# An adaLN block with differential attention on one core: the work ahead of the first exponential is laid out anew

## The chip, the cores and the metric

The kernel runs on one core of a Trainium2 chip. The metric is the device time of one execution in microseconds (us); the median over three runs counts. TensorE (PE) does the matrix products, VectorE (DVE), ScalarE (ACT) and GpSimd (POOL) the elementwise work, and SyncE (SP) issues nearly all DMAs.

## The reference, cut to what matters

The input x has 4 batch elements of 2048 tokens and 256 features. There are 32 score heads of width 8 (16 heads, two softmaxes each).

```
mod = (silu(c) @ wmod).reshape(4, 6, 1, -1)
sa, ca, ga, sb, cb, gb = (mod[:, k] for k in range(6))
ga, gb = (2 * (g >= 0) - 1) * maximum(abs(g), 0.25) for both gates
h = layernorm(x) * (1 + ca) + sa
q, k, v = h @ Wq.T * 8 ** -0.5, h @ Wk.T, h @ Wv.T          # 32, 32 and 16 heads
aw = softmax(q k^T)                                        # [32, 2048, 2048] for each element
attn = rmsnorm((aw[even] - lam * aw[odd]) @ v) * subln_w * (1 - LAMBDA_INIT)
x = x + ga * (attn @ Wo.T)
h = layernorm(x) * (1 + cb) + sb
x = x + gb * (h @ (ternary(Wf) * scale).T)
```

## The kernel before, in words

**Tiles and loops.** A batch element's 2048 tokens are taken in four chunks of 512, and its 32 score heads in eight groups of four. The main loop has 16 bodies of two groups each, four for each batch element. A body issues 256 exponentials (L644), each over 128 keys by 2 heads by 512 queries; PE makes the scores of each (L744) and adds the weighted values (L758) two steps behind. The scores lie in three slots of PSUM, so PE can be at most three exponentials ahead of ACT.

**Splits.** Queries and keys are stored as sums of three bf16 parts: the head (the value rounded), the middle (the rest rounded), and the low part. A query row also gets three rows with the split of an upper bound of its scores, the *maxima*, so that the exponential needs no running maximum. Everything passes through DRAM: `q_scr`, `k_scr`, `v_scr` for the split chunks, `m_scr` for the maxima; a group's rows are loaded from there into `queries`, `keys` and `values` (two buffers each).

**Beside the main loop.** While batch element b is in the main loop, PE, DVE, POOL and SP also make the chunks of element b+1 (kind "a" in `steps_of`, in places written out by hand) and the outputs of element b-1 (kind "e"). ACT does nothing there but exponentials. Batch element 0 has no earlier element to hide behind: its four chunks are made ahead of the main loop, and that stretch is what the change lays out anew. I call it the opening.

**The opening before.** SP loads c, the lambdas, wmod, the first chunk of x and the five weights (L420 to L427). PE makes the modulation as rows, 4 by 1536 (L653); DVE edits them (L916 to L924), SP stores them to `mod_scr` (L429), and loads them back as columns, one feature in each partition (`a_cols`, L347). DVE also makes the ternary weight (L930 to L932) and clears what it must, and then adds to `setup_done`; PE waits for it ahead of the first transpose. Then, for each chunk: transposes (L664), DVE's evacuation with the modulation (L969), queries and keys (L678), values (L670), DVE's evacuations (L971, L974) and its maxima and minima (L951 to L956). The split goes hand over hand: ACT writes the head (L635), POOL subtracts (L587), ACT writes the middle (L637), POOL the low part (L589), and only then does ACT take the next of the four pieces. `a_qk`, `a_parts` and `a_v` exist once. So ACT's first head of a chunk waits until all 13 stores of the chunk before have landed. Behind the fourth chunk come the bounds (L728), DVE's reductions and split (L1060 to L1081), four transposes (L715), DVE's copies (L1069), the stores to `m_scr` (L412) and the loads of the maxima (L405). SP loads the first group's rows (L392, L398) once the last chunk is stored.

**At a change of batch element** PE reads a flag that says whether the bounds are good enough (L780). If they are not, PE makes exact maxima in a long block of instructions; the trace shows no instruction of it, so PE always branches over it.

Of the kernel before, what the change touches and what calls it, by code (L numbers as in the profile page):

```python
# [7 lines left out]
ALU = mybir.AluOpType  # L8
# [4 lines left out]
P = 128  # L13

# [23 lines left out]
def adaln_diff_attention(nc, x, wqT, wkT, wvT, woT, lq1, lk1, lq2, lk2, subln, wfT, cT, wmod, out):  # L38
    B, T, E = x.shape
    HD = lq1.shape[0]  # L40
    VD = 2 * HD
# [44 lines left out]
    CRIT = M_STEPS - 1  # L86
# [22 lines left out]
    def steps_of(body):  # L109
# [11 lines left out]
        if b < B - 1:  # L121
            put("a", body + NC, A_TURN if turn else [spread(i) for i in range(A_STEPS)])
# [22 lines left out]
    GROUP_LOADS = 2 * 2 + 2 + 1  # L145
    ROW_LOADS = 2 * 2
# [7 lines left out]
    m_scr = nc.dram_tensor("m_scr", [B, PARTS, NS, T], BF16, kind="Internal").ap()  # L154
    attn_scr = nc.dram_tensor("attn_scr", [B, E, T], F32, kind="Internal").ap()
    mod_scr = nc.dram_tensor("mod_scr", [B, 6, E], F32, kind="Internal").ap()

    with ExitStack() as ctx:
# [16 lines left out]
        mod_sb = sb("mod_sb", [B, 6, E])  # L175
# [34 lines left out]
        a_cols = sb("a_cols", [P, 2, EC])  # L210
# [17 lines left out]
        e_cols = sb("e_cols", [P, 2, EC])  # L228
# [19 lines left out]
        m_split = sb("m_split", [P, NB, PARTS, NS], BF16)  # L248

        m_rest = w_low[:, :, :].rearrange("p c (n s) -> p (c n) s", s=NS)  # L250
        m_parts = wmod_sb[0:PARTS * NS, :, :].rearrange("p c f -> p (c f)").bitcast(BF16)[:, 0:T]

# [14 lines left out]
        consts_set = sem("consts_set")  # L267
        ident_set = sem("ident_set")
        weights_loaded = sem("weights_loaded")
        wmod_loaded = sem("wmod_loaded")  # L270
        small_loaded = sem("small_loaded")
# [3 lines left out]
        mod_product = sem("mod_product")  # L275
# [3 lines left out]
        w_total = sem("w_total")  # L279
# [14 lines left out]
        a_cols_loaded = sem("a_cols_loaded")  # L294
        a_head = sem("a_head")
        a_rest_done = sem("a_rest_done")
        a_middle = sem("a_middle")
# [41 lines left out]
        def _(sp):  # L339
# [4 lines left out]
            def a_columns(b):  # L344

                for c in range(EC):
                    sp.dma_start(a_cols[:, :, c], mod_scr[bass.ds(b, 1), 0:2, c * P:(c + 1) * P].rearrange("o k p -> p (o k)"), allow_slow_non_contiguous=True).then_inc(a_cols_loaded, DMA)  # L347

            def a_store_qk(job, b, tc, i):

                sp.wait_ge(a_split, (job + 1) * 4 + i + 1)
                c = i % 2
                for first, n in ROW_RUNS:
                    part = QK_ROWS[first]
                    if i < 2:
                        src = a_parts[:, i, part[0]:part[0] + 1, :].broadcast_to([P, n, CH])
                    else:
                        src = a_parts[:, i, 0:n, :]
# [17 lines left out]
            def e_modulation(b):  # L376
# [3 lines left out]
                for i, kind in enumerate((2, 5)):  # L380
                    sp.dma_start(e_gate[:, i, :], mod_scr[bass.ds(b, 1), kind, :].broadcast_to([P, E])).then_inc(e_mod_loaded, DMA)
# [795 lines left out]
```

## Time and profile before

| | us |
|---|---|
| median of three runs (3962.2 to 3964.03) | 3962.35 |
| profiled execution | 3960.17 |
| its span, first to last instruction | 3958.4 |
| first exponential starts | 141.70 |
| ACT busy, share of the span | 3780.8, 96% |
| PE busy, share of the span | 3756.7, 95% |
| DVE busy; POOL busy | 1199.6; 635.7 |
| granted TensorE clock, mean | 0.987 |

The page gives busy times as shares of the whole span. Two engines at 95% and more say little of which one is waited for; that is read from the waits and the timeline. The tenth of the span in which the opening lies differs from all others: PE's busy digit is 6 in the first of 40 slices and 9 later, ACT's is 1.

### The profile page before, as it was taken

What the parts mean: (1) busy time and instruction counts of PE and PEld (TensorE: products, weight loads), DVE (VectorE), ACT (ScalarE), POOL (GpSimd) and SP (SyncE); (2) the same over time, 40 slices, a digit from 0 to 9 for tenths busy, and PEclk for the clock granted to TensorE, in tenths of its full rate; (3) what the DMA queues carried; (4) which work ended last, traced back from release to release, by engine and by line L of the source; (5) the groups of instructions that cost most, each with busy time, mean ns of one, the idle gap of its engine ahead of it and who ended that gap; (6) DMA issues with size and microseconds to landing.
All of it is one profiled execution on the core that took longest, in us unless ns stands there. A gap on an engine that the chain in (4) does not pass through costs nothing.

```text
span 3958.4 us, 74927 instructions
## 1 busy us (share of the span) xinstructions
PE 3756.7 (95%) x32082; PEld 951.4 (24%) x32082; DVE 1199.6 (30%) x2778; ACT 3780.8 (96%) x4132; POOL 635.7 (16%) x402
## 2 busy tenths in 40 slices
PE   6699999999999999999999999999999999999997
PEld 3222212222222222222222222222222222211122
DVE  7332322223232332332422332322432213212133
ACT  1699999999999999999999999999999999999995
POOL 5121212112020121211111120211200101001011
PEclk8799999999999999999999999999999999999999
DMA  5412112211122212122221211221111110301101
GB/s 175 110 38 52 35 41 49 49 25 46 34 62 50 49 47 59 35 47 59 48 49 46 50 54 41 54 59 42 46 34 39 42 41 14 60 3 25 35 19 40
DMA packets 134503, 188.35 MB, mean 48 GB/s; under 512 B 15172, under 2 KB 109124, under 8 KB 133960
## 3 DMA queue, kind: packets, MB, share of 16 engines
q1 hardware_dynamic: 134152, 183.35, 19.0%
q8 instruction: 260, 4.26, 0.5%
q14 instruction: 91, 0.75, 0.1%
HBM read 97.82 MB, written 85.48 MB: 46 GB/s over the span
## 4 chain that ended last, share of the span: by engine, by line
ACT 58%; issue 28%; PE 11%; DMA 1%; POOL 1%; DVE 1%; SPq 0%; POOLq 0%; DVEq 0%; ACTq 0%
ACT probs L644 57%; PE ps L758 6%; PE ps L744 3%; PE ps L670 1%; DMA v_scr<-a_v 1%; PE ps L678 1%; POOL a_parts L589 0%; POOL a_rest L587 0%; DMA m_scr<-wmod_sb 0%; PE ps L664 0%; ACT a_parts L637 0%; DMA w_o<-in_woT_dram 0%; PE ps L728 0%; SPq L359 0%; DVE normed L886 0%
## 5 line engine op out<-in xcount | busy, mean ns | idle before, releaser
L644 ACT ACTIVATE probs<-ps 128x1024 f32<-128x1024 f32 x4096 | 3760.1, 1493 | 40.5 <-PE ps L744 39.4
L758 PE MATMUL ps<-probs,values 128*32 128x512 f32 x16384 | 2186.8, 606 | 8.2 <-DVE seg_t L1008 3.6
L744 PE MATMUL ps<-queries,keys 64*128 64x512 bf16 x8192 | 1467.5, 386 | 125.6 <-DMA queries<-m_scr 23.7
L618 POOL TENSOR_TENSOR seg_rs<-seg_ms,neg_half 64x16 f32<-64x16 f32 x128 | 370.5, 2894 | 2909.3 <-DVE seg_ms L1017 2909.3
L744 PEld LDWEIGHTS ps<-queries,keys 64*128 64x128 bf16 x8192 | 374.7, 92 | 1863.7 <-ACT probs L644 1583.3
L758 PEld LDWEIGHTS ps<-probs,values 128*32 128x32 f32 x16384 | 322.6, 108 | 572.3 <-issue 500.2
L1008 DVE STREAM_TRANSPOSE seg_t<-ps 128x512 f32<-128x512 f32 x128 | 91.8, 717 | 868.3 <-PE ps L758 868.3
L994 DVE TENSOR_TENSOR e_tmp<-ps,e_gate 128x512 f32<-128x512 f32 x64 | 44.1, 689 | 450.5 <-PE ps L670 450.5
L1021 DVE TENSOR_TENSOR seg_n<-seg_d,seg_rs 64x256 f32<-64x256 f32 x128 | 62.7, 490 | 386.5 <-POOL seg_rs L618 386.5
L971 DVE TENSOR_SCALAR a_qk<-ps 128x512 f32<-128x512 f32 x64 | 44.2, 691 | 345.0 <-PE ps L678 344.7
L1025 DVE SCALAR_TENSOR_TENSOR seg_a<-seg_n,subln_sb 32x256 f32<-32x256 f32 x256 | 133.9, 523 | 6.0
L664 PE MATMUL ps<-ident,normed 128*32 128x128 f32 x2048 | 100.3, 286 | 19.5 <-DVE stats L941 10.4
L664 PEld LDWEIGHTS ps<-ident,normed 128*32 128x32 f32 x2048 | 69.0, 116 | 146.5 <-issue 145.9
L969 DVE TENSOR_SCALAR a_hT<-ps,a_cols 128x512 f32<-128x512 f32 x32 | 25.6, 808 | 220.0 <-PE ps L664 220.0
L678 PE MATMUL ps<-a_hT,w_q 128*32 128x256 f32 x1024 | 79.2, 405 | 13.2 <-DVE a_hT L969 13.2
L1029 DVE STREAM_TRANSPOSE seg_o<-seg_a 32x512 f32<-32x512 f32 x128 | 89.5, 700 | 4.4
L670 PE MATMUL ps<-w_f,e_hT 128*32 128x256 f32 x1024 | 78.1, 388 | 6.9 <-DVE e_hT L991 6.8
L670 PE MATMUL ps<-w_o,e_attn 128*32 128x256 f32 x1024 | 77.5, 379 | 1.4 <-DMA e_x<-in_x_dram 1.3
L678 PE MATMUL ps<-a_hT,w_k 128*32 128x256 f32 x1024 | 73.5, 379 | 0.0
L670 PE MATMUL ps<-w_v,a_hT 128*32 128x256 f32 x1024 | 73.5, 379 | 0.0
L974 DVE COPY a_v<-ps 128x256 f32<-128x256 f32 x64 | 23.7, 416 | 156.6 <-PE ps L670 155.0
L991 DVE TENSOR_SCALAR e_hT<-ps,e_cols 128x512 f32<-128x512 f32 x32 | 25.7, 805 | 144.8 <-PE ps L664 144.8
(116 smaller groups left out, 1176.5 us busy)
## 6 DMA issues: line engine op xcount, KB each, us to landing
queries<-q_scr SPq DMA_DIRECT2D x64, 384.0 KB
keys<-k_scr SPq DMA_DIRECT2D x64, 384.0 KB
v_scr<-a_v SPq DMA_DIRECT2D x16, 1024.0 KB, 4.5
values<-v_scr SPq DMA_DIRECT2D x32, 512.0 KB
q_scr<-a_parts SPq DMA_DIRECT2D x32, 384.0 KB, 2.6
k_scr<-a_parts SPq DMA_DIRECT2D x32, 384.0 KB, 2.6
a_x<-in_x_dram SPq DMA_DIRECT2D x16, 512.0 KB, 12.7
q_scr<-a_parts SPq DMA_DIRECT2D x32, 256.0 KB, 2.9
```

What stands on the lines that cost most here:

```text
L618: nc.gpsimd.tensor_tensor(seg_rs[:, :], seg_ms[:, :], neg_half[0:64, :], ALU.pow).then_inc(seg_rs_done, 1)
L644: nc.scalar.activation(probs[:, u % PRING, n % PAIRS, :, :], slots[slot_of(body, n)], ACT.Exp).then_inc(exp_done, 1)
L664: last = nc.tensor.matmul(bank[j:j + 32, n * P:(n + 1) * P], src[:, n, c * P + j:c * P + j + 32], ident[:, :], start=True, stop=True)
L670: last = nc.tensor.matmul(bank[j:j + 32, (n % 2) * E:(n % 2 + 1) * E], hT[:, c, n * P + j:n * P + j + 32], w[:, c, :], start=(c == 0), sto ...
L678: last = nc.tensor.matmul(bank[j:j + 32, t], w[:, c, f * P + j:f * P + j + 32], hT[:, c, t], start=(c == 0), stop=(c == EC - 1))
L744: last = nc.tensor.matmul(slots[slot_of(body, n)][:, half, :], keys[buf][at:at + KS_ROWS, n % PAIRS, blk * P:(blk + 1) * P], queries[buf][ ...
L758: last = nc.tensor.matmul(pv[j:j + VW, :], values[buf][:, blk, half, :], probs[:, u % PRING, pair, half, :], start=(blk == 0), stop=(blk = ...
L971: last = V.tensor_scalar(a_qk[:, i - 2, :], bank, SCALING if i < 4 else 1.0, None, ALU.mult)
L1008: V.transpose(seg_t[:, :, :].rearrange("p c d -> p (c d)"), pv).then_inc(pv_read, 1)
L1021: V.tensor_tensor(seg_n[:, :, :], seg_d[:, :, :], seg_rs[:, :].rearrange("p (c o) -> p c o", o=1).broadcast_to([64, NQ, VD]), ALU.mult).th ...
L1025: last = V.scalar_tensor_tensor(seg_a[:, :, h * VD:(h + 1) * VD], seg_n[q, :, :], 1.0 - LAMBDA_INIT, subln_sb[q, :].rearrange("p (o d) -> ...
L1029: V.transpose(seg_o[:, :], seg_a[:, :, :].rearrange("p c d -> p (c d)")).then_inc(seg_done, 1)
```

## The change

What it does, part by part; numbers in brackets are used in the text below.

(1) *Modulation.* PE makes the columns themselves, eight small products with wmod as the stationary side, for the first two kinds ahead of the first transpose and for kinds 3 and 4 behind the bounds. The gates stay rows. Of wmod the first third is loaded by itself, the first chunk of x goes ahead of it, and ACT's queue issues the loads of Wq, Wk and Wv. The ternary weight, the gates and the lambdas move behind the fourth chunk, and PE no longer waits for `setup_done` ahead of the first transpose. POOL clears two of four row buffers later, and by 32-bit words.

(2) *Evacuation and split.* In the opening ACT evacuates the transposes (`turned`) and the queries and keys (`projected`), and sums the keys on the way. `hT`, the rest and the parts are double-buffered, the second `parts` in `probs`. POOL's subtraction of piece i goes ahead of its low part of piece i-1, and ACT's head of piece i ahead of its middle of i-1. PE transposes chunk tc+1 between the keys and the values of chunk tc.

(3) *First rows.* SP loads the first group's rows of chunk tc-1 in the middle of chunk tc.

(4) *Maxima.* `m_scr` and `m_split` have the head outermost, so a head's three rows are neighbours in `m_parts`, and SP loads them from there (`first_maxima`) at the opening and at each change of batch element; in the opening ACT copies them out of PSUM. The stores to `m_scr` remain, behind it. The flag's bound is now taken ahead of the split.

(5) *The branch.* PE gets a prefetch hint for the branch over the exact block, half a block of 16 units ahead of each change of batch element and once in the opening.

(6) In body 0 the steps of kind "a" stand eight units later.

```
+            turned(0)
+            for tc in range(NC):
+                projected(tc, 0)
+                for i in range(1, 4):
+                    projected(tc, i)
+                    middle(tc, i - 1)
+                if tc < NC - 1:
+                    turned(tc + 1)
+                middle(tc, 3)
...
+            for tc in range(NC):                            # POOL
+                if tc < NC - 1:
+                    a_power(tc + 1)
+                rest(tc, 0)
+                for i in range(1, 4):
+                    rest(tc, i)
+                    low(tc, i - 1)
+                low(tc, 3)
...
+            def projected(tc, i):
+                act.wait_ge(p_projected, tc * 4 + i + 1)
+                if tc > 0:
+                    act.wait_ge(p_rest_done, (tc - 1) * 4 + i + 1)
+                    act.wait_ge(p_bounded, (tc - 1) * 4 + i + 1)
...
+                if tc > 1 and i == 0:
+                    act.wait_ge(p_stored[tc % 2], 4 * len(ROW_RUNS) * DMA)
...
+            def first_rows(tc):                             # SP
+                sp.wait_ge(p_stored[tc % 2], (tc // 2 + 1) * (4 * len(ROW_RUNS) * DMA))
+                sp.wait_ge(p_v_stored, (tc + 1) * DMA)
...
-            group_rows(0, 0, 0)
-            m_stores(0)
-            group_maxima(0, 0, 0)
+            first_rows(NC - 1)
+            sp.wait_ge(p_maxima, NC)
+            first_maxima()
+            m_store(0, m_stored)
...
-                with pe.If(exact > 0):
+                pe.br_lt(exact, 1, on_true=f"pe_ready_{b}", on_false=f"pe_exact_{b}").branch_hint(skip_hint)
...
-            put("a", body + NC, A_TURN if turn else [spread(i) for i in range(A_STEPS)])
+            put("a", body + NC, A_TURN if turn else [spread(i + (body == 0)) for i in range(A_STEPS)])
```

PE's queue in the opening, where the first chunk ends and the second begins. Before (`w_q`, `w_k`, `w_v` are the weights):

```order
L678 MATMUL ps<-a_hT,w_k 32x256 x32
L670 MATMUL ps<-w_v,a_hT 32x256 x32
L664 MATMUL ps<-ident,normed 32x128 [waits a_normed]
L664 MATMUL ps<-ident,normed 32x128 x31
L678 MATMUL ps<-a_hT,w_q 32x256 [waits a_evacuated]
```

And now:

```order
L771 MATMUL ps<-a_hT,w_k 32x256 x32
L757 MATMUL ps<-ident,normed 32x128 [waits p_turned_read,a_normed]
L757 MATMUL ps<-ident,normed 32x128 x15
L757 MATMUL ps<-ident,normed 32x128 [waits p_turned_read]
L757 MATMUL ps<-ident,normed 32x128 x15
L763 MATMUL ps<-w_v,a_hT 32x256 x32
L771 MATMUL ps<-e_hT,w_q 32x256 [waits p_projected_read,p_turned_read]
```

The transposes moved ahead of the values, so the values lie between them and the product that needs their evacuation.

SP's queue in the opening, from the last store of a chunk on. Before, with what follows the fourth chunk (three stores for each of four pieces and one of `a_v` make up a chunk):

```order
L364 DMA v_scr<-a_v 128x8x256 [waits a_evacuated]
L347 DMA a_cols<-mod_scr 128x2x1 x2
L342 DMA a_x<-in_x_dram 128x4x256
L392 DMA queries<-q_scr 48x2x2048 [waits a_stored]
L392 DMA keys<-k_scr 48x2x2048
L392 DMA queries<-q_scr 48x2x2048
L392 DMA keys<-k_scr 48x2x2048
L398 DMA values<-v_scr 128x1024
L412 DMA m_scr<-wmod_sb 96x512 [waits m_evacuated] x4
L405 DMA queries<-m_scr 3x4096 [waits m_stored]
```

Now, from the second chunk's second piece on; the five loads stand in each chunk but the first, and once more at the end:

```order
L381 DMA q_scr<-probs 128x3x512 [waits a_split]
L381 DMA q_scr<-probs 128x2x512
L381 DMA q_scr<-probs 128x512
L420 DMA queries<-q_scr 48x2x512 [waits p_v_stored,p_stored0]
L420 DMA keys<-k_scr 48x2x512
L420 DMA queries<-q_scr 48x2x512
L420 DMA keys<-k_scr 48x2x512
L427 DMA values<-v_scr 128x256
L370 DMA a_x<-in_x_dram 128x4x256 [waits a_normed]
L381 DMA k_scr<-probs 128x3x512 [waits a_split]
```

The loads of the first group moved into the chunks; the load of x and the stores of the keys now stand behind their wait.

PE's queue eight units ahead of the first change of batch element, now (the scores of a unit are four products, its weighted values four more; before, the same rows stand without the hint):

```order
L851 MATMUL ps<-probs,values 32x512 [waits exp_done]
L851 MATMUL ps<-probs,values 32x512 x3
L952 BRANCH_PREFETCH_HINT
L837 MATMUL ps<-queries,keys 128x512 [waits exp_done]
L837 MATMUL ps<-queries,keys 128x512
```

Only the hint is new; the read of the flag and the branch stand behind the body's last unit as before.

## Rows read from the trace of the kernel before

**Rows 1.** The page, busy time of each engine.
```profile
PE 3756.7 (95%) x32082; PEld 951.4 (24%) x32082; DVE 1199.6 (30%) x2778; ACT 3780.8 (96%) x4132; POOL 635.7 (16%) x402
```

**Rows 2.** Waits of ACT: us in total, times, longest.
```profile
ACT probs L644 <- PE ps L744: 39.4, 12, 26.9
```

**Rows 3.** Timeline of ACT from the first exponential: start, duration, [idle before].
```profile
141.70 939.57 ACT L644 ACTIVATE probs<-ps 128x1024 f32<-128x1024 f32 x1024 [26.89 <-PE ps L744]
...
1083.91 1.94 ACT L644 ACTIVATE probs<-ps 128x1024 f32<-128x1024 f32 x2 [2.64 <-PE ps L744]
...
3907.54 7.84 ACT L644 ACTIVATE probs<-ps 128x1024 f32<-128x1024 f32 x8 [0.34 <-PE ps L744]
```

**Rows 4.** Timeline, all engines, from the start to the first store.
```profile
11.41 8.20 PE L653 MATMUL ps<-wmod_sb,silu 128*4 128x512 f32 x12 [11.41 <-DMA wmod_sb<-in_wmod_dram]
...
17.53 1.41 DVE L875 BATCH_NORM_STATS2 stats<-a_x 128x6 f32<-128x256 f32 x4
...
20.69 1.38 DVE L886 TENSOR_SCALAR normed<-a_x,moments,a_rstd 128x256 f32<-128x256 f32 x4 [1.14 <-POOL a_rstd L568]
...
30.34 3.64 PE L664 MATMUL ps<-ident,normed 128*32 128x128 f32 x64 [10.40 <-DVE stats L941]
...
34.90 3.66 PE L678 MATMUL ps<-a_hT,w_q 128*32 128x256 f32 x64 [0.92 <-DVE a_hT L969]
...
41.57 2.41 SPq L359 DMA_DIRECT2D q_scr<-a_parts  x3
```

**Rows 5.** Timeline, two chunks of the opening.
```profile
60.08 0.63 ACT L635 ACTIVATE a_parts<-a_qk 128x512 bf16<-128x512 f32 x1 [8.94 <-DMA v_scr<-a_v]
...
62.69 1.16 POOL L589 TENSOR_TENSOR a_parts<-a_rest,a_parts 128x512 bf16<-128x512 f32 x1 [0.74 <-ACT a_parts L637]
...
63.67 1.92 PE L664 MATMUL ps<-ident,normed 128*32 128x128 f32 x64
...
73.91 3.63 PE L678 MATMUL ps<-a_hT,w_k 128*32 128x256 f32 x64
```

**Rows 6.** Timeline, DVE's normalisation with POOL busy, and with POOL idle.
```profile
39.10 2.52 DVE L886 TENSOR_SCALAR normed<-a_x,moments,a_rstd 128x256 f32<-128x256 f32 x4
...
75.30 1.38 DVE L886 TENSOR_SCALAR normed<-a_x,moments,a_rstd 128x256 f32<-128x256 f32 x4
```

**Rows 7.** Timeline of SP's queue, last store to the maxima's loads.
```profile
117.81 0.67 SPq L364 DMA_DIRECT2D v_scr<-a_v  x1
...
123.81 0.35 SPq L392 DMA_DIRECT2D queries<-q_scr  x1
...
126.49 1.87 SPq L412 DMA_DIRECT2D m_scr<-wmod_sb  x4
138.40 0.56 SPq L405 DMA_DIRECT2D queries<-m_scr  x2
```

**Rows 8.** Stretches: from:to, length, each engine's busy time, PEclk, DMA share, GB/s.
```profile
0.00:17.00 17.00, 5.58 (x7) 0.86 (x8) 2.79 (x6) 1.79 (x4) 15.96 (x17) 1.00 0.63 202
60.00:81.00 21.00, 17.53 (x336) 10.18 (x332) 19.27 (x41) 5.01 (x9) 10.55 (x9) 0.92 0.70 227
75.00:78.00 3.00, 3.00 (x60) 1.67 (x56) 2.93 (x9) 0.00 (x0) 0.00 (x0) 1.00 1.03 339
1005.00:1010.00 5.00, 4.62 (x36) 0.95 (x34) 0.00 (x0) 5.00 (x7) 0.00 (x0) 1.00 0.73 141
1010.00:1015.00 5.00, 4.75 (x48) 1.32 (x45) 0.46 (x1) 5.00 (x7) 0.00 (x0) 1.00 1.05 160
1015.00:1020.00 5.00, 5.00 (x52) 1.51 (x52) 2.67 (x9) 5.00 (x7) 0.00 (x0) 1.00 1.02 233
```

**Rows 9.** Timeline of DVE, the maxima of batch element 0.
```profile
104.29 0.70 DVE L1042 TENSOR_TENSOR box_w<-head_mask,box 128x80 bf16<-128x80 f32 x4
...
116.12 2.47 DVE L1069 CAST wmod_sb<-ps 96x512 bf16<-96x512 f32 x4
```

**Rows 10.** Timeline of PE at the first change of batch element.
```profile
1083.27 1.04 PE L744 MATMUL ps<-queries,keys 64*128 64x512 bf16 x4 [3.30 <-issue]
```

More of the change, by code:

```diff
@@ L342, in a_load, with store_qk @@
                 sp.dma_start(a_x[:, :, :], x[bass.ds(b, 1), bass.ds(tc * CH, CH), :].rearrange("o (n p) e -> p (o n) e", p=P)).then_inc(a_loaded, DMA)
[L344 to L351, printed above, removed]
+            def store_qk(parts, b, tc, i, stored):
                 c = i % 2
@@ L548, in _ @@
             nc.gpsimd.tensor_copy(ident_bf[:, :], ident[:, :]).then_inc(ident_set, 1)
-            for buf in range(2):
-                nc.gpsimd.memset(keys[buf][:, :, :], 1.0).then_inc(consts_set, 1)
-                nc.gpsimd.memset(queries[buf][:, :, :], 0.0).then_inc(consts_set, 1)
             nc.gpsimd.memset(head_mask[:, :], 1.0).then_inc(ident_set, 1)
@@ new lines, in _ @@
+            for i in range(M_BOUNDS):
+                m_step(0, i, ps[:, i, :])
+            skip_hint = pe.mark_branch_hint_location()
+            pe.wait_ge(p_valued_read, NC * 2)
+            pe.wait_ge(wmod_rest_loaded, DMA)
+            pe.wait_ge(w_sum_done, 1)
+            pe.wait_ge(consts_set, 8)
+            columns((3, 4), ps[:, 6, :])
+            nc.tensor.matmul(ps[:, 6, 2 * EC * B:2 * EC * B + 1], ones[:, :], w_sum[:, :], start=True, stop=True)
+            for n, kind in enumerate((2, 5)):
+                for c in range(EC):
+                    last = nc.tensor.matmul(ps[0:B, 7, n * E:(n + 1) * E], silu[:, c, :], wmod_sb[:, c, kind * E:(kind + 1) * E], start=(c == 0), stop=(c == EC - 1))
@@ L775, in _ @@
+            last.then_inc(late_product, 1)
+            m_step(0, CRIT, ps[:, 4, :])
+            for k in range(NC):
+                m_step(0, CRIT + 1 + k, ps[:, k, :])
+            pe.wait_ge(p_maxima, NC)
+            pe.wait_ge(cols_done, 2)
+            pe.wait_ge(setup_done, 1)
+            pe.wait_ge(out_loaded, 2 * DMA)
             exact_runs = pe.alloc_register("pe_exact_runs")
@@ new lines, in _ @@
+            m_sizes(mlink)
+            for i in range(CRIT + 1):
+                m_evacuate(mlink, 0, i, ps[:, (0, 1, 2, 3, 4, 5, 4)[i], :])
+            assert mlink.count == M_LINKS, mlink.count
+            V.memset(m_mean[:, :], 0.0).then_inc(m_evacuated, NC)
+            dve.wait_ge(late_product, 1)
+            link.then(V.tensor_scalar(w_scale[:, :], ps[:, 6, 2 * EC * B:2 * EC * B + 1], 1.0 / (E * E), 1e-5, ALU.mult, ALU.max))
+            columns(2, ps[:, 6, :])
+            V.tensor_copy(mod_sb[:, :, :].rearrange("b k e -> b (k e)"), ps[0:B, 7, :])
```

473 lines of the change are left out of this document (280 added, 193 removed).

## The prediction, made before the changed kernel ran

> **What bounds the kernel now.** I read the page's busy times first, then who waits for whom, then the timeline. On the page ACT is busy 96% of the span and PE 95% [rows 1]; shares alone don't say which is waited for. ACT's timeline does: from 141.70 on the first batch element's 1024 exponentials take 939.57 us without a gap, 0.918 us each [rows 3], though PE does all projections of the next element beside them. So the exponentials set the pace, and work beside them costs nothing while PE keeps its slots full. What is left is time in which ACT has no exponential: ACT waited for PE twelve times, 39.4 us in all, 26.9 of it in one wait [rows 2], which is the end of the opening. The other 12.5 us are at the three changes of batch element, but for three small waits at the run's end such as the 0.34 us one [rows 3], some 0.9 together: 11.6 us at the changes, 2.64 of them in the first gap [rows 3]. What follows the last exponential isn't touched by more than the source of two columns. So the change can take time from two places: the 141.7 us of the opening, and the 11.6 us.
>
> **The opening, its start.** The first transpose runs at 30.34, though its input (the normalised chunk) was there at 22.07, for it waited for DVE's clearing [rows 4]. Part (1) takes that wait away, moves x to the front and sends three weights by ACT's queue. From the start of the statistics to the normalised chunk is 22.07 - 17.53 = 4.5 us [rows 4]. When x is there is not shown; the first 17 us moved 202 GB/s [rows 8], and c, x and the first third of wmod are 1.05 MB, so 5.2 us for these alone and 9.1 with the 0.79 MB of the other queue beside them. I take 7.5, and the transposes at 12, 18.3 us earlier. The modulation columns lie beside this: eight small products must beat the 8.20 us that PE took for the rows [rows 4]; if they took all of that from 8 on, they would be 2 to 3 us late. Range 10 to 16.
>
> **The opening, the chunks by compute.** Before, ACT's second head of a chunk had to wait for POOL, and its first 8.94 us for the last store to land [rows 5]. Now the pieces overlap and the buffers are double. PE has per chunk 3 x 3.63 us of products (q, k, v; only k's is shown) and 1.92 of transposes, 12.8 us [rows 5]. POOL has 8 x 1.16 + 1.0 = 10.3 [rows 5]. DVE was busy 19.27 us in a chunk of 21 [rows 8] and loses two evacuations of the transposes, four of queries and keys and two sums, all 512 columns wide; at 0.7 us (a fourth of the four 512-column copies' 2.47 us is 0.6 [rows 9]) these are 5.6, so 13.7 stay. PE and DVE are thus near each other, 13.7 us a chunk. The first query product follows the transposes by 34.90 - 30.34 = 4.6 [rows 4], so at 16.6; the fourth chunk's at 16.6 + 3 x 13.7 = 57.7; its queries, keys and values end 3 x 3.63 later, at 68.6. From the weights of the bounds to DVE's last copy was 116.12 + 2.47 - 104.29 = 14.3 us [rows 9]; ACT's copies don't change that by more than 1. From the issue of the maxima's two loads to the first exponential was 141.70 - 138.40 = 3.3 us [rows 3, 7]; four loads make it 4.1. By compute the first exponential stands at 87.0.
>
> **The opening, the chunks by DMA.** This is what I expect to be late next. A chunk's stores are four pieces of 128 x 6 x 512 bf16 and 1 MB of values, 4.19 MB. With the DMA engines full they moved 339 GB/s at a share of 1.03 [rows 8], 12.4 us a chunk. Between 60 and 81 us the share was 0.70 [rows 8]: there was room, and a chunk in 13.7 us takes it. The first group's rows were 2.1 MB; the stretch 1005 to 1020 holds such a load and one chunk of x and took 5 x (0.73 + 1.05 + 1.02) = 14.0 us of full engines [rows 8]; less 0.524 MB of x at 339 GB/s (1.5 us) that is 12.5, 3.1 for each chunk. They are slow by the byte: 160 GB/s at full share [rows 8]. Part (3) spreads them, it doesn't remove them, but only the last fourth is now behind the last store. So ahead of the last store's landing: 4 x 12.4 + 3 x 1.5 (x) + 3 x 3.1 = 63.4 us. The first store comes 41.57 - 30.34 = 11.2 us behind the first transpose [rows 4], at 23 to 24; data flow from 25. Landed: 25 + 63.4 = 88.4, with a gap or two 90; before, 123.81 [rows 7]. Then SP issues the last rows, 126.49 - 123.81 = 2.7 us [rows 7], and the maxima's loads, 4.1 us to the exponential: 96.8. Before, this last leg was 141.70 - 123.81 = 17.9 us, since the stores to `m_scr` stood behind the rows' loads (issued at 126.49, and their load only at 138.40 [rows 7]); part (4) takes that passage through DRAM away. DMA ends later than compute, so it decides: 96.8, 44.9 us earlier. Bounds: 84 if DMA is never the limit and DVE no slower than PE (87.0 - 3 x 0.9); 113 if stores go out at the pace of before, when the first went at 41.57 and the last at 117.81 [rows 4, 7]: 24 + 76.2 + 6 to land + 2.7 + 4.1.
>
> One thing may make the chunks longer. DVE's normalisation took 2.52 us where POOL worked beside it and 1.38 where POOL was idle [rows 6], 1.14 more, one POOL operation. Eight operations of this kind (four normalising, four making `q_sign`) could each wait once in a chunk: 8 x 1.16 = 9.3 us at most, as against the few waits that the 19.27 us already hold. I take 1 to 2 us more per chunk, which DMA covers: it has 9.8 us of slack over compute in four chunks. The Trainium skill, page SBUF — State Buffer, section Who interferes with whom, says that this pair of ports is an exclusive lock and that the second to come blocks for a whole instruction; the trace agrees, 1.14 against 1.16 us. By it the upper of the two numbers is possible, since POOL is now busy most of a chunk.
>
> **The changes of batch element.** PE issued nothing for 3.30 us at the branch [rows 10], and ACT, a little ahead of it by its slots, stood 2.64 us; the next scores then ran at 1.04 us for four matmuls, and ACT waited some more, until 11.6 us in three changes. Part (5) hints the branch. If the 3.30 us are the fetch of the target, they go, save for the read of the flag; I take 9 of 11.6 us. The trace has no hint, so the ends are 0 and 11.6. The Trainium skill, page Runtime: NRT & Kernel Launch, section Instruction fetch mechanics, says that fetch runs ahead in order only, and that a taken branch to a page not held must wait for a DMA. That agrees with a wait of 3.30 us with no releaser; it speaks of no hint, and by it alone nothing is gained here.
>
> **What costs nothing.** (6) and the moved loads of columns lie beside exponentials whose pace of 0.918 us hid such work already [rows 3]. What moved behind the fourth chunk (ternary weight, gates, lambdas) follows the maxima on DVE and must be done before the last rows land, 10 us later; without that cover it would cost its few us. In the opening the branch lies under the DMAs.
>
> **Sum.** The profiled execution is 3960.17 us, 1.77 more than its span. 3960.17 - 44.9 - 9 = 3906.3. The median of the runs is 2.2 us above the profiled one: 3908.5, I say 3908.
>
> **The rivals.**
> *Hint without effect* (chance 0.22). For: PE may wait at the read of the flag and not for instructions; the trace can't tell. Against: no releaser is named. 3908.5 + 9 = 3917.
> *DMA isn't the limit* (0.12). For: loads in pieces of 1 KB may go at 339 GB/s, as stores do (3 x 1.6 us saved), and the stores may start earlier. Against: the 160 GB/s. First exponential at 86 to 90, 3898 to 3902.
> *POOL and DVE block each other* (0.18). If all eight operations wait, 13.7 + some 6 = 19.7 a chunk: 16.6 + 3 x 19.7 + 10.9 + 14.3 + 4.1 = 105; or SP's one queue, in which the stores of keys and the load of x now stand behind the wait for the chunk before, delays both, up to 113. 3917 to 3925.
> *Slower* (0.03). The exact block. Bounds now come from sums taken by ACT and in another order; if a bound of one element rose above 80, the flag would be set. Then DVE reduces 512 times over 2048 columns, each at least 4 x 0.6 us by the copy [rows 9]: 1.2 ms, about 5100 us. It decides from one flagged element on. Against: only rounding differs, and the trace has no instruction of that block. *No change* (0.03): the opening as long as before for a reason I don't see.
>
> **How the numbers follow.** My forecast, DMA-bound with a hint that works, has 0.42 (3902 to 3914). The range for 8 in 10 takes in the missing hint and most of the blocked case: 3898 to 3922. A measurement of this kernel tells 0.2%, about 8 us, from no change; every case but the last two lies 37 us or more below. Faster 0.94, same 0.03, slower 0.03.
>
> **What would show it.** The first exponential at about 97, and a DMA share near 1 from 30 to 90 us; the last `v_scr` store landed about 90; gaps of ACT under 1 us at the changes. Wrong, if ACT's first exponential comes with DMA share well under 0.9 in the chunks (then compute or SP's order is the limit), if PE still shows an idle time of 3 us there, or if the exponentials take more than 0.92 us.

## The result, and the profile after

| | before | after |
|---|---|---|
| median of the runs | 3963.19 us (3962.2 to 3964.97) | 3916.55 us (3916.12 to 3917.69, 4 runs) |
| ratio to before, with its 95% interval | 1 | 0.9883 [0.987, 0.9895] |
| profiled execution, its span | 3960.17, 3958.4 us | 3916.22, 3914.5 us |
| first exponential | 141.70 us | 108.32 us |
| ACT's waits for scores, the first left out | 12.5 us | 1.6 us |

The kernel is 46.6 us faster. The forecast was 3908, with a range of 3898 to 3922: the time is inside it, 8.5 us above the forecast. The span is 43.9 us shorter: 33.4 in the opening (forecast 44.9) and 10.5 behind the first exponential (forecast 9). The 10.5 are a difference: from the first exponential to the ones behind ACT's last gap it takes 3753.8 us instead of 3765.8, 12.0 less, and what follows them takes 52.4 instead of 50.9, 1.5 more. The last product of PE is the reason for the 1.5:

```profile
3904.00 5.54 PE L763 MATMUL ps<-w_f,e_hT 128*32 128x256 f32 x64 [0.92 <-DVE e_hT L1124]
```

In the kernel before, the same product took 3.66 us, at a granted clock of 0.95 (3949 to 3953). Here, from 3904 to 3908, the granted clock was 0.52, near the lower of its two levels (1.2 GHz). PE had done the same just before in both, transposes of 3.64 us behind an idle time of 6.26, so why the clock was lower here is not shown.

Waits of ACT in the kernel after (us in total, times, longest), which answers to [rows 2]:

```profile
ACT probs L736 <- PE ps L837: 11.4, 6, 9.8
```

Its timeline from the first exponential to the last gap (start, duration, count, idle before), which answers to [rows 3]:

```profile
108.32 5.61 ACT L736 ACTIVATE probs<-ps 128x1024 f32<-128x1024 f32 x6 [9.83 <-PE ps L837]
114.29 1.94 ACT L736 ACTIVATE probs<-ps 128x1024 f32<-128x1024 f32 x2 [0.36 <-PE ps L837]
116.53 3657.09 ACT L736 ACTIVATE probs<-ps 128x1024 f32<-128x1024 f32 x3986 [0.30 <-PE ps L837]
...
3862.13 7.83 ACT L736 ACTIVATE probs<-ps 128x1024 f32<-128x1024 f32 x8 [0.34 <-PE ps L837]
```

From 116.53 on 3986 exponentials run without one gap, over all three changes of batch element; 3657.09 / 3986 = 0.917 us each, the pace of before. The 1.6 us of waits that are left lie elsewhere: 0.66 right behind the first exponential, and the same 0.93 at the run's end as before. Nothing that was laid beside them cost time.

The opening's timeline, all engines, chosen rows, which answer to [rows 4] and [rows 5]:

```profile
10.13 6.21 DVE L1021 TENSOR_SCALAR normed<-a_x,moments,a_rstd 128x256 f32<-128x256 f32 x4 [1.21 <-POOL a_rstd L608]
...
16.49 3.64 PE L757 MATMUL ps<-ident,normed 128*32 128x128 f32 x64 [4.59 <-DVE normed L1021]
...
28.69 4.19 SPq L381 DMA_DIRECT2D q_scr<-a_parts  x6
32.92 0.64 SPq L370 DMA_DIRECT2D a_x<-in_x_dram  x1
38.31 1.41 DVE L1010 BATCH_NORM_STATS2 stats<-a_x 128x6 f32<-128x256 f32 x4 [3.82 <-DMA a_x<-in_x_dram]
40.41 1.11 POOL L608 TENSOR_TENSOR a_rstd<-a_ve,neg_half 128x4 f32<-128x4 f32 x1 [5.64 <-DVE a_ve L1015]
41.63 4.78 DVE L1021 TENSOR_SCALAR normed<-a_x,moments,a_rstd 128x256 f32<-128x256 f32 x4
46.47 3.64 PE L757 MATMUL ps<-ident,normed 128*32 128x128 f32 x64 [6.14 <-DVE normed L1021]
...
64.76 3.44 PE L757 MATMUL ps<-ident,normed 128*32 128x128 f32 x64 [3.89 <-DVE normed L1021]
```

Two things are to be seen. The first normalisation took 6.21 us, where 1.38 was its time with POOL idle [rows 6], and the transposes start at 16.49 instead of 12. And PE then stands still twice, 6.14 and 3.89 us, for the normalised chunk (I call these places the seams): SP issues the load of x only at 32.92, behind the six stores of queries; DVE's statistics wait for it until 38.31, POOL's power (which makes `a_rstd`, the factor of the normalisation) until 40.41, and four DVE operations take 4.78 us beside POOL's splits.

Stretches (length, busy time of PE, PEld, DVE, ACT and POOL, PEclk, DMA share, GB/s), which answer to [rows 8]:

```profile
30.00:90.00 60.00, 46.99 (x843) 31.90 (x835) 47.82 (x102) 27.39 (x52) 34.91 (x30) 0.89 0.88 287
75.00:85.00 10.00, 7.02 (x133) 3.69 (x125) 8.65 (x16) 6.18 (x14) 9.06 (x8) 1.00 1.07 368
99.00:103.00 4.00, 0.00 (x0) 0.00 (x0) 2.63 (x9) 0.00 (x0) 1.01 (x1) 0.50 0.22 59
```

Over the 60 us the DMA engines' share was 0.88, by stretches of 15 us 0.93, 0.88, 0.78 and 0.95: near full, with a dip where PE stands still at the second seam. The prediction's sign of being wrong was a share "well under 0.9"; 0.88 doesn't decide that. What does speak against the forecast is the first exponential, at 108.32 instead of about 97, and the last store. SP's queue at the end of the opening, which answers to [rows 7]:

```profile
93.30 0.68 SPq L385 DMA_DIRECT2D v_scr<-a_v  x1
99.52 0.34 SPq L420 DMA_DIRECT2D queries<-q_scr  x1
99.90 0.43 SPq L420 DMA_DIRECT2D keys<-k_scr  x1
100.38 1.91 SPq L420 DMA_DIRECT2D queries<-q_scr  x1
102.33 0.43 SPq L420 DMA_DIRECT2D keys<-k_scr  x1
102.80 0.43 SPq L427 DMA_DIRECT2D values<-v_scr  x1
103.28 2.91 SPq L452 DMA_DIRECT2D queries<-wmod_sb  x4
```

The last store landed at 99.5, since SP's wait for it ended then, not at 90; from there to the first exponential it is 8.8 us, not 6.8. So the 11.5 us that the opening misses are 4.5 (start) + 5.0 (chunks) + 2.0 (last leg). Counted from one store of values to the next, against before: the first store of values was issued 16.4 us earlier (38.88 for 55.30), the three chunks from there to the last took 54.4 instead of 62.5 us, and from the last one's issue to the first exponential it was 15.0 instead of 23.9.

### The profile page after: what moved, and what is told of

Same layout as the page of the kernel before. It is cut to its first block, busy times and chain, and to the rows that moved or that the text cites. A ratio compares the mean times of both kernels' runs of the same rounds, so it can differ in the third digit from the quotient of the medians.

```text
span 3914.5 us, 75013 instructions
## 1 busy us (share of the span) xinstructions
PE 3750.6 (96%) x32110; PEld 960.2 (25%) x32110; DVE 1188.5 (30%) x2745; ACT 3797.7 (97%) x4168; POOL 628.2 (16%) x402
## 4 chain that ended last, share of the span: by engine, by line
ACT 58%; issue 29%; PE 11%; DVE 1%; POOL 1%; SPq 0%; DMA 0%; ACTq 0%; POOLq 0%; DVEq 0%
ACT probs L736 58%; PE ps L851 5%; PE ps L837 3%; PE ps L763 1%; PE ps L771 1%; PE ps L757 0%; DVE normed L1021 0%; SPq L381 0%; PE ps L821 0%; SPq L420 0%; DMA v_scr<-a_v 0%; DMA a_x<-in_x_dram 0%; DVE seg_t L1141 0%; POOL a_rest L641 0%; POOL probs L647 0%
## 5 line engine op out<-in xcount | busy, mean ns | idle before, releaser
L1104 DVE TENSOR_SCALAR a_qk<-ps 128x512 f32<-128x512 f32 x48 | 33.2, 692 | 341.2 <-PE ps L771 341.2
L1102 DVE TENSOR_SCALAR a_hT<-ps,cols_sb 128x512 f32<-128x512 f32 x24 | 19.4, 810 | 213.7 <-PE ps L757 213.7
L1124 DVE TENSOR_SCALAR e_hT<-ps,cols_sb 128x512 f32<-128x512 f32 x32 | 25.7, 804 | 144.9 <-PE ps L757 144.9
L771 PE MATMUL ps<-a_hT,w_q 128*32 128x256 f32 x896 | 66.3, 379 | 1.0 <-ACT a_hT L692 1.0
## 6 DMA issues: line engine op xcount, KB each, us to landing
a_x<-in_x_dram SPq DMA_DIRECT2D x16, 512.0 KB, 12.9
```

What stands on the lines that cost most here:

```text
L771: last = nc.tensor.matmul(bank[j:j + 32, t], w[:, c, f * P + j:f * P + j + 32], hT[:, c, t], start=(c == 0), stop=(c == EC - 1))
```

## The experiments

Each is the kernel after with one edit, unless said otherwise. "Measured" gives the median with its range and the ratio to before with its 95% interval. Medians are to be read beside 3916.55, the profiled execution's first exponential beside 108.32.

Two things blur small differences. The kernel before, measured beside these runs, took 3959.7 us (the first four runs), 3962.86 (the next four), 3961.88 (the three after them) and 3963.31 (the last), and 3963.19 beside the kernel after; so medians of different groups can be compared to 3 or 4 us only. And the end of the run differs from kernel to kernel: what follows ACT's last gap took 52.4 to 52.9 us in the profiled executions of the kernel after and of the runs with clears late, values twice, and clears, x and maxima, whose last product of PE took 5.3 to 5.7 us, and 50.4 to 51.0 in all others, where it took 3.66. That has nothing to do with the edits as they were meant, and puts up to 2 us into the times. I therefore go by the traces' opening where a difference is small.

**The hint of the branch taken out.**

```
-  pe.br_lt(exact, 1, on_true=..., on_false=...).branch_hint(skip_hint)
+  pe.br_lt(exact, 1, on_true=..., on_false=...)
```

> The changed kernel without the branch hints, all else as it is. Theory (the idle time at the changes of batch element was the fetch of the branch's target): the idle time of PE of some 3.3 us comes back at each of the three changes, with the slow matmuls behind it, and the time rises by 9 to 12 us over the changed kernel's 3916.5, to 3926 to 3928. Rival (the gaps went for another reason, such as the earlier flag or the steps that moved): under 2 us. In the opening neither expects a difference, since the branch lies under the DMAs there; first exponential at 108.3.

Measured: 3927.59 us (3926.39 to 3931.68), ratio to before 0.9921 [0.9904, 0.9937], 11.0 more than with the hint, as the theory had it. ACT's waits, and PE at the first change of batch element:

```profile
ACT probs L736 <- PE ps L837: 22.0, 16, 6.9
```

```profile
1049.35 0.61 PE L837 MATMUL ps<-queries,keys 64*128 64x512 bf16 x4 [2.99 <-issue]
```

The idle time of [rows 10] is back, with no releaser, here and at the other two changes (3.42 and 2.93 us), and ACT's waits at the changes sum to 13.4 us, where they were 11.6 before and are none with the hint. The hint is the whole gain behind the opening; the rival by which PE waits at the read of the flag falls, for the flag is read in both. The Trainium skill, page Runtime: NRT & Kernel Launch, section Instruction fetch mechanics, lets a taken branch wait for the fetch of its target: the trace agrees, 2.99 us without the hint and no gap with it. By that page alone nothing was to be had.

**POOL's later clears behind the first normalisation.**

```
   a_power(0)
+  pool.wait_ge(a_normed, 1)
   clear(keys[1], ONE_PAIR)
```

> The changed kernel with one more wait: POOL's second block of clears comes behind DVE's first normalisation instead of beside it. Theory (DVE's four operations were held off by POOL's clears, one each): the normalisation takes 1.4 us instead of 6.2, the first transpose runs at 11.7 instead of 16.5, and if the DMAs or the chunks' own length set what follows, all of it moves with it: first exponential at 103 to 105, 3 to 5 us less in total. Rival (what sets the end is fixed by the load of the next chunk of x, which waits for the loads of the weights): the first exponential moves by under 1.5 us.

Measured: 3911.59 us (3911.05 to 3913.34), 0.9879 [0.9863, 0.9896]; 5.0 less. The normalisation and the transposes:

```profile
10.15 1.38 DVE L1022 TENSOR_SCALAR normed<-a_x,moments,a_rstd 128x256 f32<-128x256 f32 x4 [1.21 <-POOL a_rstd L608]
...
11.97 3.64 PE L758 MATMUL ps<-ident,normed 128*32 128x128 f32 x64
```

The four operations take 1.38 us again, the transposes start at 11.97, where the forecast had them, and the first exponential comes at 103.04, 5.3 earlier. That is what the theory expected, and the rival by which the load of x sets the end falls. In the kernel after, POOL's clears of 1.80, 1.80 and 1.95 us ran from 10.05 to 15.49, beside the four DVE operations: the first of these, begun at 10.13, ended at 13.74, just behind the second clear (13.59), and the next at 15.63, just behind the third. So a memset of POOL, too, holds DVE back until the whole instruction is done, and the first operation had to let two of them pass. The Trainium skill (SBUF — State Buffer, Who interferes with whom) states such a lock; the trace agrees, 6.21 against 1.38 us.

**The values stored twice** (the second time to a buffer that nobody reads; 1 MB more for each chunk, and the other engines' work as it was; whoever waits for the values' store waits for both).

```
   store_v(0, tc, p_v_stored)
+  sp.dma_start(v_twin[...], a_v[...]).then_inc(p_v_stored, DMA)
```

> The changed kernel with each chunk's values stored a second time, to a tensor that nobody reads: 1.05 MB or 3.1 us of full DMA engines more per chunk. Theory A (DMA is the limit through the whole opening): the first exponential comes 4 x 3.1 = 12.4 us later, at 120.7. Theory B (late loads of x and POOL's order hold the chunks, DMA only the end): the slack in the chunks takes half of it, 3 to 8 us, 111 to 116.

Measured: 3923.4 us (3921.4 to 3925.49), 0.9907 [0.989, 0.9923]; first exponential at 116.94, 8.6 later, DMA share from 30 to 90 us 0.93 at 306 GB/s. The 8.6 us can't all be put down to the second store, for part of them had come before one was issued:

```profile
21.74 5.64 PE L774 MATMUL ps<-a_hT,w_q 128*32 128x256 f32 x64 [0.98 <-ACT a_hT L695]
...
42.13 0.81 SPq L386 DMA_DIRECT2D v_scr<-a_v  x1
```

The first chunk's query product took 5.64 us, where it took 3.66 in the kernel after, and the first store of values went out at 42.13 instead of 38.88, 3.3 us later. The trace gives no reason for the long product; the granted clock was 1.00 in both. From that first store to the first exponential it was 74.8 us, 5.4 more than the 69.4 of the kernel after. So of about 12.4 us more of DMA work 5.4 came through, as theory B has it (3 to 8); the rest went into the gaps of the queues. DMA is near its limit but not at it.

**The first rows loaded at the end, as before: part (3) undone.**

```
-                        if tc > 0:
-                            first_rows(tc - 1)
...
-            first_rows(NC - 1)
+            for i in range(2):
+                sp.wait_ge(p_stored[i], 2 * (4 * len(ROW_RUNS) * DMA))
+            sp.wait_ge(p_v_stored, NC * DMA)
+            group_rows(0, 0, 0)
```

> The changed kernel with part (3) undone: the first group's rows are loaded whole behind the last store, as before. Theory A (DMA is full, so that spreading only moves its work): the last store of the values lands some 9 us earlier than 99.5, the rows take 12.5 us behind it, first exponential at 105 to 109, no change within 3 us. Theory C (spreading hides 9 us under the chunks): first exponential at 115 to 118, 7 to 10 us more in total. Theory B (the wait for the stores in the middle of SP's queue makes the load of x late): the idle times of PE at the ends of chunks, 6.1 and 3.9 us, shrink by more than half in the second.

Measured: 3915.91 us (3913.08 to 3918.17), 0.9892 [0.9875, 0.9908]; first exponential at 107.34. This is theory A's number, and theory C (115 to 118) falls: the part is worth nothing here. The last store of values is issued at 85.56, 7.7 us earlier than with the rows between, and the leg from there to the first exponential is 21.8 us instead of 15.0. The rows' bytes are in the way in one place or in the other. But the edit changes more than the place of the bytes. Without the rows ahead of it the last chunk of x is asked for 3.0 us earlier (49.20), and PE's second idle time falls from 3.89 to 1.93 us, as theory B expected. What the rows in the middle cost as bytes, and what they cost by holding up the load of x behind them, this run doesn't separate; nor was part (3) undone with x asked for early, where it may be worth something.

**The load of x behind the first split's stores.**

```
-  if i == 1: first_rows(tc - 1); wait; a_load(tc + 2)
+  if i == 0: wait; a_load(tc + 2)
+  if i == 1: first_rows(tc - 1)
```

> The changed kernel with the load of the next chunk of x issued by SP behind the chunk's first piece, no longer behind the second piece and the wait for the chunk before. Theory B (x comes late and holds DVE's statistics, with them POOL and the transposes): the loads are issued 2.5 to 5 us earlier, PE's idle times of 6.1 and 3.9 us at the chunks' ends fall by 2 to 4 each, and the first exponential comes 2 to 4 us earlier than 108.3, less than the idle times shrink, since DMA (a share of 0.88 from 30 to 90) takes part of it. Theory A (DMA is the only limit): the idle times shrink, the first exponential moves by under 1 us.

Measured: 3909.01 us (3908.19 to 3909.94), 0.9863 [0.9846, 0.9879]; 7.5 less. PE at the two seams:

```profile
43.56 3.50 PE L756 MATMUL ps<-ident,normed 128*32 128x128 f32 x64 [3.19 <-DVE normed L1020]
...
59.46 1.96 PE L756 MATMUL ps<-ident,normed 128*32 128x128 f32 x64 [1.92 <-DVE normed L1020]
```

x is asked for at 30.99, 44.38 and 60.59 instead of 32.92, 52.22 and 71.65, PE's waits are halved (from 10.0 to 5.1 us), the share from 30 to 90 us is 0.93, and the first exponential comes at 102.88, 5.4 earlier. Theory A (under 1 us) falls, and the gain is more than theory B's 2 to 4. Of the 5.4 the three chunks give 3.8 (50.6 us from the first to the last store of values, for 54.4) and the last leg 1.6 (13.5 for 15.0). The median's 7.5 hold another 2 that lie in the run's end (50.4 for 52.4 us) and not with x. SP's order was the larger part of the 5 us of the chunks.

**POOL's power for the next chunk behind two splits instead of ahead of them.**

```
-  if tc < NC - 1: a_power(tc + 1)    (ahead of rest(tc, 0))
+  if i == 1 and tc < NC - 1: a_power(tc + 1)    (behind low(tc, 0))
```

> The changed kernel with POOL's power for the next chunk behind the first low part, no longer ahead of the chunk's first subtraction. Theory B (the power waits for the statistics of a late x, and the splits wait behind it): POOL's idle times of 5.6 and 6.9 us ahead of the splits of chunks 1 and 2 go, the first stores of chunk 1 go out some 5 us earlier than 44.99, DMA is busier from 38 to 45 us, and the first exponential comes 2 to 5 us earlier. Rival (the splits lock out DVE's normalisation, which makes the transposes later still): the idle times of PE grow from 6.1 and 3.9 us, first exponential within 1 us or later.

Measured: 3923.29 us (3921.49 to 3925.52), 0.99 [0.9884, 0.9917]; first exponential at 115.86, 7.5 later. PE at the seams, of which there are now three:

```profile
33.97 3.64 PE L757 MATMUL ps<-ident,normed 128*32 128x128 f32 x64 [6.14 <-DVE normed L1021]
...
55.19 3.64 PE L757 MATMUL ps<-ident,normed 128*32 128x128 f32 x64 [6.15 <-DVE normed L1021]
...
76.09 3.64 PE L757 MATMUL ps<-ident,normed 128*32 128x128 f32 x64 [6.19 <-DVE normed L1021]
```

The edit was meant to take away POOL's 5.64 us of waiting in front of the splits, and the first exponential was to come 2 to 5 us earlier. A miss: the rival, by which PE's idle times grow, is what came. The power comes late, the normalisation behind it (29.13, again 4.78 us) too, and PE waits 6.1 to 6.2 us at each of three seams, where it waited at two. POOL's wait was the cheaper one.

**The maxima's copies ahead of the last rows.** SP's order is `first_maxima()`, then `first_rows(NC - 1)`.

> The changed kernel with the four loads of the maxima issued ahead of the wait for the last stores, no longer behind the last rows. The maxima are in SBUF at 98.5 and the last store has landed at 99.5, so the four issues (2.9 us) lie under the wait. Theory (SP's issues in a row are the last leg): the first exponential comes 2 to 3 us earlier, 105.3 to 106.3. Rival (the landing of the last rows, slow by the byte, is what ends last and the maxima's issues lay under it): under 1 us.

Measured: 3915.42 us (3914.03 to 3917.28), 0.988 [0.9863, 0.9896]. From the last store of values to the first exponential 12.9 us instead of 15.0, as the theory had it (2 to 3 us), but the first exponential at 108.35 in the profiled execution, whose last store of values went out 2.1 us later (95.44 for 93.30). That delay was there ahead of the edit's place: the first query product took 5.50 us instead of 3.66, and the first stores went out at 30.61 instead of 28.69. The median's 1.1 us less are undecided by themselves.

**Four edits together** (clears late, x early, power late, maxima first).

> The changed kernel with all four edits of these experiments: POOL's clears behind the first normalisation, the load of x early, POOL's power behind the first low part, the maxima's loads ahead of the last rows. If the gains added up: 5.3 (measured for the clears) + 3 + 3 + 2.5 = 14, first exponential at 94. Theory A, with DMA as the floor: the stores start at 24.4, 63 us of full DMA engines bring the last landing to about 89 at best, first exponential 96 to 98, time 3904 to 3907. Rival (DVE and POOL lock each other out more as they are packed closer): 100 or later, 3909 or more.

Measured: 3919.99 us (3918.18 to 3921.34), 0.9889 [0.9873, 0.9906]; first exponential at 114.42. A clear miss of theory A, by 13 to 16 us; the rival (100 or later, 3909 or more) holds. The late power spoils the others. With it x is asked for only after a normalisation that is itself late: at 29.85, 51.16 and 72.11, where the run with clears and x below has 28.39, 42.15 and 58.81.

**The maxima through DRAM at the start: part (4) undone there.**

```
-  first_maxima()
   m_store(0, m_stored)
+  sp.wait_ge(m_stored, NC * DMA)
+  group_maxima(0, 0, 0)
```

> The first group's maxima go out to DRAM with the four stores and are loaded back from there by two loads, as in the kernel before; the copies inside SBUF at the first group are gone, all else is as after. Theory A (the copies inside SBUF replace a store that must land and a load behind it, and this chain is the last leg before the first scores): the chain becomes four stores, their landing (some 4 us by the copies' own landing, 106.2 to 107.6 in the kernel after), two loads and their landing again, so the first exp comes 4 to 6 us later, at 112 to 114, and the run takes 3920 to 3923. Theory B (the rows of the last chunk, which stand ahead of the maxima in SyncE's program, land as late as the copies, so the maxima are not last): the stores overlap the rows' landing, the first exp moves by less than 2 us, and the run stays at 3916 to 3918.

Measured: 3917.26 us (3914.89 to 3918.95), 0.9888 [0.9871, 0.9904]. SP's queue, and the first scores:

```profile
103.27 1.88 SPq L457 DMA_DIRECT2D m_scr<-wmod_sb  x4
106.67 0.58 SPq L441 DMA_DIRECT2D queries<-m_scr  x2
...
109.24 1.04 PE L838 MATMUL ps<-queries,keys 64*128 64x512 bf16 x4 [11.31 <-DMA queries<-m_scr]
```

The way through DRAM costs 1.6 us of the first exponential (109.89) and nothing that the medians can tell: theory A (4 to 6 us) fails, theory B (under 2) holds. Before, from the issue of these stores to their load it was 11.9 us [rows 7], which the prediction put down to the passage; here it is 3.4. In those 11.9 us the DMA engines' share was 0.95 at 189 GB/s, with the rows' 2.1 MB issued just ahead. So they were in the main the rows' bytes, and they are short now because only a fourth of the rows is left there. That `m_scr` is also laid out otherwise was not tested apart.

**Clears and x together.**

> Two edits together that each took 5 to 7 us by themselves: the second clears on POOL wait for the first normed chunk, and the loads of x(tc + 2) are issued behind the stores of the chunk's first split instead of its second. Theory A (the two delays lie in a row, so they add): first exp 5.3 and 5.4 us earlier than 108.32, at 97.6, and 3904 to 3906. Theory B (the x loads come early enough only because the DMA queues are not full; with the whole stretch 4 us shorter they are, and the last stores land no earlier than the backlog lets them): the DMA share between the first store and the last is 0.97 or more, first exp 100 to 103, and 3906 to 3909.

Measured: 3905.64 us (3904.54 to 3908.96), 0.9859 [0.9843, 0.9876]; 10.9 less. First exponential at 100.33. Stretch:

```profile
30.00:90.00 60.00, 47.46 (x831) 31.63 (x823) 51.70 (x118) 26.87 (x53) 33.02 (x29) 0.91 0.95 314
```

8.0 of the 10.7 us add up in the first exponential. The 2.7 that don't were lost ahead of the chunks and not in full queues: the first query product took 5.84 us (3.66 with the clears alone), and the first stores went out at 26.75 instead of 24.18. From the first to the last store of values it is 50.5 us and from there to the first exponential 13.4, both as with x early alone. The two edits' gains thus add, which is theory A's mechanism: the median lies in its 3904 to 3906, and the share of 0.95 stays under theory B's 0.97. The first exponential stands among theory B's 100 to 103 only by what the start lost.

**Clears, x and the maxima's copies first.**

> The edits of the run with clears and x, and the copies of the maxima issued ahead of the last chunk's rows. Theory A (what the first scores wait for is the landing of whichever DMA is issued last, and the copies, 2 KB and slow to land, gain from going first): the leg from the last store of v to the first exp is 2 us shorter than with those two edits alone, and the run 1.5 to 2.5 us shorter. Theory B (the order of the two does not matter, since both must land and their sum is the same): within 1 us of the run with the two edits.

Measured: 3904.29 us (3902.53 to 3906.5), 0.9853 [0.9837, 0.987]. Share 0.96, first exponential at 98.13, and from the last store of values to it 11.7 us for 13.4. In the profile that is nearly the first theory (2 us); the medians differ by 1.4 us, with intervals that overlap. Its first query product took 5.51 us, too. It is the fastest version run, 12.3 us below the kernel after, and its first exponential is 1.3 us from the 96.8 that the forecast worked out for full DMA engines.

**A chunk split only when the one before has landed: the overlap undone.**

```
-  if tc > 1 and i == 0: act.wait_ge(p_stored[tc % 2], ...)
+  if tc > 0 and i == 0: act.wait_ge(p_stored[(tc - 1) % 2], ...); act.wait_ge(p_v_stored, tc * DMA)
```

> ACT's first piece of every chunk after the first waits until all stores of the chunk before have landed, as in the kernel before, though the buffers stay double; all else is as after. In the kernel after, the last store of a chunk was issued at 38.88, 57.85 and 78.04 and the next chunk's first piece was made at 35.84, 56.46 and 74.15. Theory A (the second buffer lets a chunk be split while the one before is still stored, and this carries the shorter chunks: 54.4 us from the first to the last store of values instead of 62.5): the first piece would have to wait until some 5 us behind the store of values, at 44, so each of the three chunks is 6 to 9 us longer, the first exp stands at 122 to 130, and the run takes 3930 to 3939. Theory B (each chunk already waits some 5 us at its seam for the normalised x, and the wait for the landed store lies beside that wait): 1 to 3 us a chunk, first exp 111 to 117, the run 3919 to 3926.

Measured: 3931.78 us (3929.09 to 3934.25), 0.9921 [0.9905, 0.9938]; first exponential at 122.94, 14.6 later. ACT's first pieces of the three chunks:

```profile
44.97 0.63 ACT L709 ACTIVATE probs<-a_qk 128x512 bf16<-128x512 f32 x1 [9.22 <-DMA v_scr<-a_v]
...
68.45 0.63 ACT L709 ACTIVATE a_parts<-a_qk 128x512 bf16<-128x512 f32 x1 [12.47 <-DMA v_scr<-a_v]
...
93.58 0.63 ACT L709 ACTIVATE probs<-a_qk 128x512 bf16<-128x512 f32 x1 [13.86 <-DMA v_scr<-a_v]
```

Both numbers lie in theory A. The wait of [rows 5] is back, and the share falls to 0.75. From the first store of values to the last it is 70.4 us (38.78 to 109.14), 16.0 more, while the last leg gets 1.2 shorter. Of the parts undone here this is the largest; part (1), behind which the first store of values goes out 16.4 us earlier than before, was not undone.

## Why the prediction was right, and where 8.5 us went

**Right: what bounds the kernel.** The exponentials' pace didn't move (0.917 us), and both places named gave all that was gained. The time is in the range, and the sign of the gain is as forecast, 46.6 us of 54. But the forecast's own case, a first exponential at about 97 and 3902 to 3914 us, did not come. The time is inside by the width of the range, which was taken to hold most of the blocked case.

**Right: the changes of batch element.** Taken as 9 us of 11.6; all 11.6 came, for no gap is left at a change. A part had been left standing for the read of the flag, and ACT shows no gap for it. The exponentials beside those gaps, which had been slower, add 1.1, and new waits behind the first exponential take 0.7 off; that makes 12.0, so the term was too small by 3.0; the slower end of the run takes 1.5 of them back.

**Wrong by 4.5 us: the start.** The transposes were set at 12 with 4.5 us from the start of the statistics to the normalised chunk, a duration from a time when POOL was idle [rows 4, 6]. But the change moves POOL's clears to just that place. The prediction counted the lock for the chunks, at one POOL operation of 1.16 us each, and not here, where the operations are memsets of 1.8 us. The move of the clears brought 4.5 us back.

**Wrong by 5.0 us: the chunks.** The step that failed is "which DMA covers: it has 9.8 us of slack over compute in four chunks", that is, that DMA's time hides what DVE and SP lose. It takes the bytes as one block that only has to be pushed through. They come in bursts: PE stood 6.14 and 3.89 us, stores came late for it, and the share was 0.88. The rival "POOL and DVE block each other", which has SP's queue order in it as well (0.18, first exponential at 105 to 113, 3917 to 3925) named both mechanisms; the first exponential at 108.32 is its number, the time 3916.55 lies just under it. x asked for earlier brought 3.8 us of it back in the chunks, and 1.6 in the last leg. The other half of PE's waits is argued only: PE waited for the normalisation each time, and that took 4.78 and 3.81 us where 1.38 is its time with POOL idle, 5.8 more in two seams. That this lock takes the rest of a seam was not separated: the one edit that tried to move POOL's operations made it worse. With clears, x and maxima mended the share is 0.96 and the first exponential at 98.13. So the DMA bound is borne out to 1.3 us by that version, and the kernel as changed didn't reach it.

**Wrong by 2.0 us: the last leg.** The issue of the rows took 3.7 us instead of 2.7, since one of the loads took 1.91 (at most 0.43 for the others). And from the first of the maxima's four loads to the first exponential it was 5.0 us instead of 4.1; that term came from a row in which all other loads had landed, while here the rows' bytes are still under way. The copies issued first make it shorter by 1.7 to 2.1 us.

**Right in sum, wrong in its reason: parts (3) and (4).** The leg did fall by 8.9 us against before. The prediction put this down to the last fourth of the rows and to the passage through DRAM. Undone alone, neither costs anything the medians can tell (3915.91 and 3917.26 against 3916.55). Part (3) moves 7 us from the leg into the chunks; part (4) is worth 1.6 us, and the 11.9 us of [rows 7] that it was to remove were in the main the rows' bytes. What carries the opening is the overlap of part (2), 14.6 us, and, by the trace alone, the earlier start of part (1). Whether each is worth more in before than when undone here was not tried.

**The medians.** The profiled execution is 0.3 us below the median here, where 2.2 were added. With the terms above: 3906.3 + 11.5 - 3.0 + 1.5 = 3916.3, measured 3916.22.

## What to carry to other kernels

A total of DMA time is a bound for a stage only if the queues are fed all the time: follow one chunk through the program of the engine that issues, and look where the load for the next chunk stands behind stores that wait for this one. When an engine's work is moved, price its neighbour on the shared port at the new place, not at the old one. An idle engine (POOL's 5.64 us) is not always the one to serve; ask first whose input that wait protects. And before a difference is put down to an edit, look whether it begins at the edit's place: here up to 3.3 us were lost ahead of it, most of them in one product, and up to 2 behind it, in the end of the run.

## What the runs showed of the hardware that was not expected

- With the hint, the branch left no idle time: at three changes PE's 2.9 to 3.4 us each, 11.0 us in the medians, are gone.
- POOL's memsets, which only write, hold DVE's normalising operations back as its arithmetic does: four operations took 6.21 us beside three memsets of 1.8 to 1.95, 4.78 us beside splits of 1.2, and 1.38 alone.
- A product of 64 matmuls of 128x256 took 3.66 us in most places and 5.3 to 5.8 in others. At the run's end the granted clock was 0.52 (kernel after); in the first chunk it was 1.00, and the reason stays open.
- A stretch of mostly stores moved 368 GB/s at full share (1.07), more than the 339 of [rows 8].
